# Graph network kernel, first stage: six beats of preparation per superblock, finished tiles handled at other places, a table load split in three

## The reference

```python
# x (3125, 256); src, dst (103125,): both directions of 50000 edges and a loop per node, sorted by dst
h = relu(layernorm(x))
def conv(h, W, b):                       # three of these: W1, W2 with relu, W3 without
    return segment_sum((h @ W)[src] * norm, dst) + b      # norm = dinv[src] * dinv[dst], one more loop per node
x = x + conv(relu(conv(relu(conv(h, W1, b1)), W2, b2)), W3, b3)
h = relu(layernorm(x))
red = segment_sum(h[src] + relvectors[edge_type], dst)
x = x + gru_cell(red, h, w_ih, w_hh, b_ih, b_hh)
```

## Time and profile before

| | |
|---|---|
| median of 3 runs | 934.55 us (934.06 to 934.75) |
| profiled execution, its own time | 933.93 us |
| its span, first to last instruction | 930.0 us |
| PE busy | 886.0 us, 95% of the span |
| VectorE, ScalarE, GpSimd busy | 444.3, 290.0, 75.5 us |
| mean granted clock of TensorE | 0.992 |

### The profile page before, as it was taken

One profiled execution on the slowest core, in us unless ns is written; L12 is line 12 of the kernel. 1 busy time (PEld: TensorE's weight loads), 2 busy tenths in 40 slices (PEclk: granted clock), 3 DMA queues, 4 the chain that ended last, 5 costly groups with the idle time before them and its releaser, 6 DMA issues.

```text
span 930.0 us, 16580 instructions
## 1 busy us (share of the span) xinstructions
PE 886.0 (95%) x5495; PEld 529.4 (57%) x5495; DVE 444.3 (48%) x1164; ACT 290.0 (31%) x609; POOL 75.5 (8%) x244
## 2 busy tenths in 40 slices
PE   2779999999999999999999999999999999999996
PEld 1348777777777865444444544445464455555553
DVE  7956888888887201021112413336253133334345
ACT  3365566666666311011111202222231111222122
POOL 0210111000000025551000000000000000000000
PEclk9989999999999999999999999999999999999999
DMA  6100000000000410000000101111401000000101
GB/s 191 30 2 2 4 22 17 16 16 22 17 16 16 144 32 3 3 3 1 1 0 24 44 14 39 46 46 51 137 20 31 10 25 24 23 23 23 30 28 31
DMA packets 37009, 28.50 MB, mean 31 GB/s; under 512 B 12870, under 2 KB 35554, under 8 KB 36925
## 3 DMA queue, kind: packets, MB, share of 16 engines
q1 hardware_dynamic: 36252, 26.97, 9.6%
q10 hardware_dynamic: 672, 0.41, 0.2%
HBM read 17.56 MB, written 9.81 MB: 29 GB/s over the span
## 4 chain that ended last, share of the span: by engine, by line
PE 92%; DVE 5%; issue 1%; ACT 1%; SPq 0%; DMA 0%; DVEq 0%
PE ps L1233 42%; PE ps L905 12%; PE ps L807 10%; PE ps L642 9%; PE ps L1244 5%; PE ps L646 5%; PE ps L1263 2%; PE ps L886 2%; DVE node_b L914 1%; PE ps L842 1%; PE ps L854 1%; PE ps L874 1%; PE ps L627 1%; PE ps L818 0%; DMA count<-in_dst 0%
## 5 line engine op out<-in xcount | busy, mean ns | idle before, releaser
L1233 PE MATMUL ps<-count,node_b 128*128 128x512 f16 (+3 forms) x1400 | 270.5, 351 | 0.4 <-DVE node_b L1395 0.3
L807 PE MATMUL ps<-node_b 128*128 128x175 f16 x808 | 192.9, 259 | 13.7 <-issue 7.8
L1233 PEld LDWEIGHTS ps<-count,node_b 128*128 128x128 f16 (+2 forms) x1400 | 121.5, 98 | 142.1 <-issue 7.3
L905 PE MATMUL ps<-node_a,count 128*128 128x256 f16 x1050 | 200.7, 277 | 0.2 <-DVE node_a L1026 0.2
L914 DVE TENSOR_TENSOR node_b<-node_b 128x1024 f16<-128x1024 f16 (+2 forms) x303 | 161.7, 587 | 0.0
L1109 ACT ACTIVATE count<-ps 128x500 f32 x202 | 122.8, 608 | 96.7 <-PE ps L807 94.9
L1233 PE MATMUL ps<-count,node_a 128*128 128x512 f16 (+2 forms) x700 | 134.7, 352 | 0.0
L807 PEld LDWEIGHTS ps<-node_b 128*128 128x128 f16 x808 | 79.8, 99 | 62.7 <-issue 28.4
L905 PEld LDWEIGHTS ps<-node_a,count 128*128 128x128 f16 x1050 | 101.1, 100 | 4.2 <-ACT count L1109 0.4
L1233 PEld LDWEIGHTS ps<-count,node_a 128*128 128x128 f16 (+1 forms) x700 | 60.0, 97 | 73.9 <-issue 7.1
L1325 DVE SCALAR_TENSOR_TENSOR work<-ps,dinv,params 128x256 f32<-128x256 f32 (+1 forms) x25 | 12.0, 480 | 125.0 <-PE ps L1244 125.0
(11 more groups left out here) (210 smaller groups left out, 787.9 us busy)
## 6 DMA issues: line engine op xcount, KB each, us to landing
node_a<-in_x SPq DMA_DIRECT2D x4, 768.0 KB, 8.4
table_scratch<-agg SPq DMA_DIRECT2D x21, 128.0 KB, 1.8
node_b<-table_scratch SPq DMA_DIRECT2D x3, 768.0 KB, 6.6
xt<-x_scratch SPq DMA_DIRECT2D x16, 128.0 KB, 2.1
out<-scaled SPq DMA_DIRECT2D x16, 128.0 KB, 1.7
xt<-in_x SPq DMA_DIRECT2D x12, 128.0 KB, 2.0
params<-in_x SPq DMA_DIRECT2D x12, 128.0 KB, 2.0
x_scratch<-xt SPq DMA_DIRECT2D x12, 128.0 KB, 1.7
```

The source lines that it names most:

```text
L807: return PE.matmul(window(s)[:, :, keys], low, key_hot[k][:, j, :, i].rearrange("p (t w) -> p t w", w=SPAN), start=(s == 0 and j == 0), st ...
L905: last = PE.matmul(out_slot(u)[0:m, :], count[:, t, u * P:u * P + m], node_a[:, t, part, :], start=(t == 0 and part == 0), stop=(t == T - ...
L1233: last = PE.matmul(ps[:, b, 0:cols], nodes[0:k, t, part, f * P:(f + 1) * P], count[0:k, t, c * CHUNK:c * CHUNK + cols], start=(n == 0 and ...
```

## The change

Numbers first. `BEATS` goes from 4 to 6, so that preparation takes fewer superblocks, and `PRODUCTS_FROM` comes out as 12 instead of 18. `COUNTS_AT` 24 to 23, `WEIGHT_AT` 28 to 26, `SCALE_AT` 33 to 32, `WEIGH_AT` 40 to 36, `FACTORS_AT` 42 to 38, the histogram gets a beat of its own (30); `LOW_PART_AT` stays one pair behind `WEIGH_AT`, which is now 12 beats. `out_shape_act` moves from 5 to 3 superblocks behind, `out_low_dve` from 9 to 12. The offset words are loaded 11, 8, 7, 7 and 8 at a time, the last three ahead of the waits of superblocks 2, 4 and 6. VectorE makes the rows of pair 0 ahead of the branch, around its wait for the verdict. GpSimd clears the tail before the loops of tile 0 instead of behind them.

```diff
-OFFSET_LOADS, LAST_WORDS_AT = (11, 18, 12), 4
+OFFSET_LOADS, WORDS_AT = (11, 8, 7, 7, 8), (2, 4, 6)
-BEATS = 4
+BEATS = 6
...
             DVE.tensor_reduce(verdict[:, :], rules, AX_X, ALU.add).then_inc(verdict_summed, 1)
+
+            DVE.wait_ge(keys_out, 5)
+            rank_and_source_rows(0)
             DVE.wait_ge(judged, 1)
             DVE.tensor_copy(verdict_i[:, :], ps[0:1, 5, 0:1]).then_inc(verdict_in, 1)
+            key_rows(0)
...
-        COUNTS_AT = 24
+        COUNTS_AT = 23
...
-        WEIGHT_AT = 28
-        SCALE_AT = 33
+        HIST_AT = 30
+        WEIGHT_AT = 26
+        SCALE_AT = 32
         DEGREE_AT = 36
-        WEIGH_AT = 40
-        FACTORS_AT = 42
+        WEIGH_AT = 36
+        FACTORS_AT = 38
         AHEAD_ACT = 2
-        LOW_PART_AT = WEIGH_AT + 8
-        OUT_AT, OUT_LOW_AT = 5, 9
+        LOW_PART_AT = WEIGH_AT + BATCH * BEATS
+
+        OUT_AT, OUT_ACT_AT, OUT_LOW_AT = 5, 3, 12
...
-        PRODUCTS_FROM = (WEIGH_AT + T) // BEATS + 2
+        PRODUCTS_FROM = max((WEIGH_AT + T) // BEATS + 2, SETTLE_FIRST + 1)
...
+                if s in WORDS_AT:
+                    offset_words.extend(load_offsets(2 + WORDS_AT.index(s)))
                 PE.wait_ge(hot_made, s // BATCH + 1)
                 if s + 1 >= RING:
                     PE.wait_ge(win_written, s + 2 - RING)
-                if s == LAST_WORDS_AT:
-                    offset_words.extend(load_offsets(2))
...
                 for u in range(EARLY):
-                    if s == summed_at[u] + OUT_AT:
+                    if s == summed_at[u] + OUT_ACT_AT and summed_at[u] + OUT_AT < NS:
                         out_shape_act(u)
...
             POOL.partition_all_reduce(fours[:, 2:5], bounds[:, 4:7], P, RMAX).then_inc(small_reduced, 1)
+
+            POOL.wait_ge(x_weighted, T)
+            POOL.memset(node_a[:, T - 1, :, :], 0.0).then_inc(tail_cleared, 1)
             POOL.wait_ge(ident16_made, 1)
             for u in range(EARLY):
                 POOL.wait_ge(win_written, settled(u))
                 loops(ALU.add, u, u + 1, POOL).then_inc(tile_looped, 1)
-                if u == 0:
-
-                    POOL.wait_ge(x_weighted, T)
-                    POOL.memset(node_a[:, T - 1, :, :], 0.0).then_inc(tail_cleared, 1)
```

More of the change, by code:

```diff
@@ L261, in spread, with one_hot, rank_and_source_rows, key_rows @@
             return v.rearrange("(p d) -> p d", p=1).to_broadcast([P, v.shape[0]])
+        hot_made = sem("hot_made")
+        def one_hot(to, keys, first, width):
+            n = keys.shape[1]
+            iota = iota2[:, 2 * first:2 * (first + width)].rearrange("p (k j) -> p k j", j=2).unsqueeze(1).to_broadcast([P, n, width, 2])
+            return DVE.tensor_tensor(to, iota, keys.unsqueeze(2).to_broadcast([P, n, width, 2]), ALU.is_equal)
+        def rank_and_source_rows(m):
+            k, two = m % PAIRS_KEPT, slice(BATCH * m, BATCH * (m + 1))
+            one_hot(rel_rank_hot[BATCH * m // GROUP % 2][:, :, m % 2, :, :], rel_rank_k[:, :, two], 0, WINDOW).then_inc(*dve_seq.up())
+            one_hot(low_hot[k], low_k[:, :, two], 0, P).then_inc(*dve_seq.up())
+            one_hot(carry_hot[k].unsqueeze(1), carry_k[:, two].unsqueeze(1), 1, T).then_inc(*dve_seq.up())
+        def key_rows(m):
+            one_hot(key_hot[m % PAIRS_KEPT], key_k[:, :, BATCH * m:BATCH * (m + 1)], 0, T * SPAN).then_inc(hot_made, 1)
         def load_rows(engine, row, of, got):
@@ L731, in program, with rows_for, pair_of @@
         HIGH_AT = LOW_AT + 2 * Q
-        WEIGHT_AT = 28
-        SCALE_AT = 33
+        HIST_AT = 30
+        WEIGHT_AT = 26
+        SCALE_AT = 32
         DEGREE_AT = 36
-        WEIGH_AT = 40
-        FACTORS_AT = 42
+        WEIGH_AT = 36
+        FACTORS_AT = 38
         AHEAD_ACT = 2
-        LOW_PART_AT = WEIGH_AT + 8
-        OUT_AT, OUT_LOW_AT = 5, 9
-        assert HIGH_AT < WEIGHT_AT and WEIGHT_AT // BEATS * BEATS + BEATS <= DEGREE_AT - BEATS and TURN_AT + T <= WEIGH_AT
+        LOW_PART_AT = WEIGH_AT + BATCH * BEATS
+        OUT_AT, OUT_ACT_AT, OUT_LOW_AT = 5, 3, 12
+        def rows_for(beat):
+            return (beat // BEATS + 1) // BATCH
+        def pair_of(beat):
+            return beat // (BATCH * BEATS)
+        assert HIGH_AT < WEIGHT_AT and TURN_AT + T <= WEIGH_AT and WINDOW <= COUNTS_AT < HIST_AT < WEIGH_AT
+        assert all(pair_of(own) >= rows_for(of_pe) for own, of_pe in ((COLUMNS_OUT_AT, COLUMNS_AT), (WEIGHT_AT, COUNTS_AT), (DEGREE_AT, HIST_AT)))
         assert SCALE_AT + SCALE_STEPS <= FACTORS_AT < BEATS * ASIDES // (WINDOW - 1)
-        PRODUCTS_FROM = (WEIGH_AT + T) // BEATS + 2
+        PRODUCTS_FROM = max((WEIGH_AT + T) // BEATS + 2, SETTLE_FIRST + 1)
         early_products = [(u, t, part) for u in range(EARLY) for t in range(T) for part in range(2)]
@@ L824, in build_pe @@
                         beside_pe(w)
[L825 to L833, removed]
                 for u, t, part in due[len(between) * (QUARTERS - 1) // QUARTERS:]:
@@ L887, in beside_pe @@
                 last.then_inc(x_weighted, 1)
+            if beat == HIST_AT:
+                PE.wait_ge(hist_due, 2)
+                for w in range(WINDOW):
+                    for q in range(Q):
+                        part, pair = divmod(w, WINDOW // 2)
+                        last = PE.matmul(HIST, low_of[q][part][0:lanes(q), pair // 2, :, pair % 2],
+                                         high_of[0:lanes(q), (q * WINDOW + w) // 2, :, w % 2],
+                                         start=(w == 0 and q == 0), stop=(w == WINDOW - 1 and q == Q - 1), skip_group_check=True)
+                last.then_inc(degrees_done, 1)
             if beat == COLUMNS_AT:
```

15 lines of the change are left out of this document (5 added, 10 removed).

## The result

| | before | after |
|---|---|---|
| median | 934.65 us (934.06 to 935.07, 4 runs) | 941.72 us (939.0 to 942.54, 4 runs) |
| profiled execution, its own time; span | 933.93 us; 930.0 us | 939.0 us; 935.0 us |

The ratio is 1.0071, with a 95% interval of 1.0049 to 1.0093: the change makes the kernel 7 us slower. 941.0 was forecast.

What follows compares the result with a forecast made beforehand. The prediction took TensorE's instruction issue to bound the kernel. Terms -2.9 + 0.3 - 1.1 + 5.5 + 4.6, with F at nothing, gave +6.4 us on the 934.55 median: 941.0 us, range 933.0 to 944.0.

Steps and rivals of the forecast that it cites:

- A: Start up to TensorE's counts: three superblocks fewer and less waiting for words, 2.9 us earlier, bounds 1.0 to 4.5.
- B: Counts to the first low part: a loss of 0.3 us, bounds +1.5 and -2.
- C: First low part to the end of the x products: fewer sources in the open, 1.1 us saved.
- D: End of x products to first early product: GpSimd's switch back, taken at 5.55 us, makes it 5.5 us longer.
- E: Loop behind the first product: six superblocks more at 0.77 us each, 4.6 us longer.
- Rival 1: GpSimd's switch back is free, so the last low part sets the first product: 935.8 us; chance 0.24.
- F: Finished tiles' new places: VectorE's 26.5 us of waits for ScalarE go, worth nothing because TensorE's issue covers them.
- Rival 2: VectorE's waits hold TensorE in the loop; without them superblocks fall to 1.02 us, some 918 us; chance 0.04.
- Rival 3: First stage gains more and the switch is short or free: products 7 us sooner, 932.4 us and below; chance 0.11.

Runs made afterwards that it cites:

- again: The changed kernel itself, unaltered, run and profiled a second time: 941.38 us, ratio 1.0079 to the kernel before.
- loops first: Changed kernel with GpSimd's clearing moved back behind tile 0's loops: 934.97 us, ratio 1.0007 to the kernel before.
- words back: Kernel before with four beats and the change's other parts, but the last offset words in one load at superblock 4 again: 934.13 us, ratio 0.9995.
- products from 18: Changed kernel with early products from superblock 18 on instead of 12: 937.87 us, ratio 1.0036 to the kernel before.
- clear first: Kernel before with only the clearing moved ahead of the configuration row and tile 0's loops: 941.42 us, ratio 1.0079.
- 22 tiles: The kernel of 932.32 us with 22 finished tiles instead of 21, so 50 more products in the loop: 927.36 us, ratio 0.9922 to the kernel before.
- by beats: Two kernels with 22 finished tiles and three or two beats a superblock instead of four: 924.0 us and 919.55 us.
- places: Kernel before with only the finished tiles' new places: 934.03 us, ratio 0.9998.
- fixed spans: Kernel before with a superblock's three computed offsets made constants from superblock 24 on, counts misplaced: 912.62 us, ratio 0.9762.
- four beats: The kernel with 22 finished tiles, still at four beats a superblock like the kernel before: 927.36 us, ratio 0.9922.
- two beats: The kernel with 22 finished tiles, with two beats a superblock instead of four: 919.55 us, ratio 0.9835 to the kernel before.
- the kernel of 932.32 us: Kernel before with the verdict's pair 0, spread word loads and finished tiles' places, keeping four beats and loops first: 932.32 us, ratio 0.9973.

## Why the prediction was right, term by term

The forecast of 941.0 us was right to 0.7 us, and its cause was right too: the switch behind the clearing and the six superblocks more in the loop. That it was as near as 0.7 us is partly luck: three terms were mis-sized (A, D, E), and their errors nearly cancel. In us against the kernel before, minus is earlier:

| term | predicted | after | again |
|---|---|---|---|
| A, to the counts | -2.9 | -5.6 | -3.8 |
| B, to the first low part (71.63 before; 65.69 and 67.62) | +0.3 | -0.3 | -0.3 |
| C, to the end of the x products | -1.1 | -1.6 | -1.6 |
| D, to the first product | +5.5 | +6.2 | +6.2 |
| E, the loop | +4.6 | +6.6 | +6.6 |
| sum; last window moved by | +6.4 | +5.3 | +7.1 |

**A was under-sized for an execution at full clock, and about right for the slowest.** Pair 1 came 0.7 us later in the first execution (31.90 for 31.17), near the 0.9 predicted. From there to the counts before took 25.3 us, after 18.9, again 20.4 and in loops first 21.4, where 3.8 less than before was predicted. The words gave 1.8 (words back) instead of 1.1. The rest, 4.6 after and 3.1 again, is that of three superblocks fewer and of the clock, which these runs don't separate; I took the superblocks at 0.9 us each, and again, whose clock of 0.96 is that of before, makes it 1.0 each. The bounds (1.0 to 4.5) hold again and loops first (-2.8), and not the first execution, which had no stretch at 1.2 GHz.

**B and C** were right within 0.6 us, B with the wrong sign: a small gain and no loss. A part of that is a slip: 56.48 - 2.9 is 53.6, and B was worked out from counts at 53.9. With 53.6 it would have been 0 and the forecast 940.7. The bounds of A and B also add up to 944.6 at the upper end, where 944 is recorded. Nor was the reduction's preparation over ahead of the maxima, as I had it:

```profile
53.55 0.39 POOL L1529 PARTITION_ALL_REDUCE fours<-bounds  x1 [5.48 <-DVE bounds L1058]
```

The maxima were ready at 52.64, the reduction began 0.9 us later, 5.5 us behind its configuration (48.1) as in the earlier trace rows, and VectorE waited 1.33 us for it. Whether it was held by the maxima or by its preparation isn't settled; in products from 18 and in loops first the profile puts the same idle time (5.64 and 5.89 us) down to "issue", which speaks for the preparation.

**D was right, and slightly small**: the way back costs 6.9 us, not 5.55 (6.97 and 7.00 after, 6.84 in clear first, 6.89 in products from 18), and the loops 0.41, not 0.98. The Trainium skill (GPSIMD Engine Reference, "Instruction dispatch") has about 6 us for a first call to a freshly loaded kernel; the runs show a price of that size for the way back too, 6.8 to 7.0, a little above it. Rival 1, a free switch, falls: with the switch hidden the kernel takes 934.97, near that rival's 935.8. Why the configuration at L290 showed no such price (my reason was that it changed nothing) no run tested.

**E was mis-sized by 2.0 us, in both executions alike, and by its working.** "0.77 us for a superblock's own part" came of giving register operations their recorded 36 and 53 ns, 0.37 us, and spreading all other time over the matmuls, 0.067 each. The runs show the opposite division: 0.006 us for a product (22 tiles) and 6.57 / 6 = 1.09 us for a superblock (1.09 again, 1.01 and 1.17 by beats; with the loop's spread, 0.95 to 1.17). By these, 1.09 + 5.56 x 0.006 = 1.12, the pace but for 0.02. Where the time is, the sequencer's rows of a single superblock after show, 201.25 to 202.22 us:

```profile
L839 PEldq ALU_OP  x6: 36/36/36, 201.3 to 202.2; - x6
...
L839 PEldq FUSED_REGOPS  x2: 52/52/53, 201.5 to 202.0; - x2
```

Eight operations start between 201.3 and 202.2, with a semaphore among them, though each is recorded for 36 or 52 ns. Taken one by one from the trace (before and after alike, 130 to 270 us, medians), the three of an offset start 0.097 us apart, and 0.13 us pass from the third to the next operation. That is 3 x 0.324 = 0.97 us a superblock and, with about one semaphore operation of 0.13, 1.1: it fits 1.09. The products' weight loads and matmuls start in between, and 22 tiles shows that more of them cost next to nothing. That the gap belongs to each register operation was not tried by itself. The Trainium skill (TensorE: Matmul & The Clock Gate, "Wait — 56ns, not 53.3ns?") gives its 62 ns a matmul for a sequencer that decodes matmuls in software, and as a bound only where the array's work is shorter. Here 50 more matmuls cost 0.006 us each and a product takes the array 0.111 us, so that price doesn't bind in this loop. That it was near my 67 ns came of dividing by the wrong count.

**F was right.** 26.5 us of VectorE's waits were worth nothing (places), for the reason given: TensorE's issue covers them. Rival 2 falls with it, and fixed spans show that VectorE and ScalarE can follow a pace of 1.04 us a superblock; VectorE could hardly follow a faster one, and with TensorE's issue out of the way its waits might count.

**Rival 3**, more gained in the first stage, was half true: the x products end 7.5 us sooner (5.7 again), more than the 3.7 I counted, but D takes 6.2 of it. Without D the changed kernel is level with before (loops first), since six superblocks more in the loop eat what the shorter preparation gives.

What stays open: which of TensorE's array and VectorE holds 1.04 us once an offset is fixed (a superblock has 5.56 x 256 + 4 x 175 + 25 + 80 columns; at the 0.111 us that 256 columns take behind the loop this is an estimated 0.97 us), and what decides whether an execution has its stretch at 1.2 GHz before the counts.

## What to carry to other kernels

Before sizing work in a loop, find what one iteration costs and what one matmul costs as two unknowns, from two stretches or two kernels with different counts; a recorded duration isn't the distance to the next instruction. Where register operations hold the issue, as here, matmuls in their gaps are almost free, so put more of them there. An engine's change of configuration belongs where a long wait follows it anyway, so that no other engine waits for the work behind it: moving one clearing of 0.52 us ahead of the switch cost 7 us. And a fixed cost per iteration is cheapest in the stage that waits for something else: more superblocks beside the preparation, not fewer, made this kernel 7.8 us faster (from four beats to two), half of the 15.5 us by which the best kernel here beats the one before.

## What was not expected of the hardware

- GpSimd's configuration row is over in 11 ns and the next ordinary operation starts 6.8 to 7.0 us after it, in four profiled executions of three kernels. In the kernel with two beats, where the row (82 ns there) follows the reduction directly and no clearing stands ahead of it, the same wait shows, with nothing waited for:

```profile
59.75 0.79 POOL L1518 PARTITION_ALL_REDUCE fours<-bounds  x1 [5.54 <-ACT count L1123]
67.46 0.41 POOL L936 TENSOR_TENSOR count<-count,ident 128x128 f16<-128x128 f16 x1 [6.93 <-issue]
```

  So the price is that of the switch and not of the clearing. Ahead of the reduction, the way there, it is 5.5 us after and 5.6 again, and up to 6.0 in the other runs. Where a longer wait follows the row, its cost can't be seen at all.
- The same 128x128 add of GpSimd took 0.41 us while VectorE stood still, 0.98 to 0.99 and 3.11 us elsewhere, and in the kernel of 932.32 us, while VectorE made pairs back to back, 4.93. It ended at 104.32, just after VectorE's first pause (from 104.04):

```profile
99.39 4.93 POOL L936 TENSOR_TENSOR count<-count,ident 128x128 f16<-128x128 f16 x1 [3.42 <-ACT count L1123]
```

```profile
102.47 1.57 DVE L270 TENSOR_TENSOR node_b<-node_b 128x1024 f16<-128x1024 f16 x3
104.20 0.33 DVE L270 TENSOR_TENSOR params<-node_b 128x320 f16<-128x320 f16 x1 [0.16 <-PE ps L828]
```

  The 3.11 us of products from 18 ended in the same way, at 98.67 with VectorE's pause from 98.39. No run took VectorE's pairs away to try it.

- A matmul of 256 columns, 0.111 us behind the loop, added 0.006 us (no more than the loop's own spread) to a loop whose issue was held by register operations.
